# Attention kernel: P by V in blocks of four key tiles instead of two, V made over six steps, and a new order of the first-pass scores

## What is computed

```python
xn = layernorm(x)                                   # (16, 56, 128)
q, k, v = xn @ qw.T + qb, ctx @ kw.T + kb, ctx @ vw.T + vb
scores = einsum('bhqd,bhkd->bhqk', q * 8 ** -0.5, k)
scores = where(mask == 0, -1e9, scores)
out = einsum('bhqk,bhkd->bhqd', softmax(scores), v)
x = x + tanh(g_xattn) * (out @ ow.T + ob)
x = x + tanh(g_ffn) * ffn(layernorm(x))             # 8 experts, top 2, and a shared one
```

## Time and profile before

| | |
|---|---|
| median of 3 runs | 525.68 us (525.66 to 526.95) |
| the profiled execution | 525.51 us, its span 523.7 us |
| PE busy | 473.9 us, 90% of the span |
| PEld busy | 351.7 us, 67% |
| DVE busy | 399.2 us, 76% |
| ACT busy | 329.6 us, 63% |
| POOL busy | 160.5 us, 31% |

### The profile page before, as it was taken

How to read it: one execution, slowest core, us unless ns; L and a number is a source line. 1 busy time by engine, 2 the same in 40 slices (tenths; PEclk the granted TensorE clock), 3 DMA queues, 4 the chain that set the end, 5 groups by cost and what they waited for, 6 DMA issues and landing times.

```text
span 523.7 us, 15766 instructions
## 1 busy us (share of the span) xinstructions
PE 473.9 (90%) x6779; PEld 351.7 (67%) x6779; DVE 399.2 (76%) x784; ACT 329.6 (63%) x422; POOL 160.5 (31%) x142
## 2 busy tenths in 40 slices
PE   1547699999999999999999999999989989999993
PEld 0214377867778686777768677786868856777772
DVE  7339477877877887787788787778867768888776
ACT  2311366666676666667666666766665788877872
POOL 4034326061532606153351615335194200000000
PEclk9959799999999999999999999999999999999998
DMA  5899986996979688796969869684500300221001
GB/s 165 179 254 195 245 193 134 250 200 165 192 173 202 147 184 177 165 199 169 207 134 197 173 162 197 173 171 105 120 3 2 84 2 25 57 73 51 3 1 35
DMA packets 39805, 72.82 MB, mean 139 GB/s; under 512 B 4638, under 2 KB 26271, under 8 KB 39736
## 3 DMA queue, kind: packets, MB, share of 16 engines
q1 hardware_dynamic: 38456, 70.90, 60.6%
q10 hardware_dynamic: 1280, 0.92, 0.7%
HBM read 24.28 MB, written 0.46 MB: 47 GB/s over the span
## 4 chain that ended last, share of the span: by engine, by line
PE 78%; DVE 7%; DMA 5%; ACT 3%; issue 3%; SPq 1%; POOL 1%; ACTq 0%; DVEq 0%
PE ring L342 16%; PE pv L382 16%; PE st L363 11%; PE ring L324 8%; PE ring L286 7%; PE st L858 7%; PE ring L911 6%; DMA ctxT<-in_ctx 4%; DVE max_part L536 2%; ACT v_ext L469 2%; DMA ident_h<-in_c_ident_h 2%; PE pv L911 2%; SPq L268 1%; PE ring L307 1%; PE ring L350 1%
## 5 line engine op out<-in xcount | busy, mean ns | idle before, releaser
L536 DVE TENSOR_REDUCE max_part<-ring 112x1 f32<-112x512 f32 (+1 forms) x384 | 244.9, 675 | 73.4 <-PE ring L342 73.2
L489 ACT ACTIVATE probs<-st 128x896 f32<-128x896 f32 x192 | 172.5, 916 | 73.5 <-PE st L363 71.4
L342 PE MATMUL ring<-keys,qrs 121*112 121x512 f16 (+1 forms) x384 | 149.7, 391 | 6.8 <-DVE max_part L536 3.3
L363 PEld LDWEIGHTS st<-qrs,keys 121*128 121x128 f16 (+1 forms) x1536 | 97.2, 102 | 29.5 <-issue 8.9
L363 PE MATMUL st<-qrs,keys 121*128 121x112 f16 (+1 forms) x1536 | 106.7, 213 | 1.0 <-ACT qrs L478 1.0
L382 PE MATMUL pv<-probs,v_ext 128*32 128x168 f32 (+3 forms) x3072 | 93.6, 262 | 0.1
L382 PEld LDWEIGHTS pv<-probs,v_ext 128*32 128x32 f32 (+1 forms) x3072 | 73.1, 109 | 21.7 <-issue 11.3
L342 PEld LDWEIGHTS ring<-keys,qrs 121*112 121x112 f16 x384 | 49.9, 130 | 41.7 <-DVE max_part L536 17.7
L614 POOL TENSOR_TENSOR k_hi<-k_raw,zero 128x512 f16<-128x512 f32 (+1 forms) x45 | 45.8, 1018 | 86.7 <-ACT k_raw L457 86.7
L286 PE MATMUL ring<-ctxT,w_qkv 128*128 128x512 f32 (+1 forms) x94 | 53.6, 656 | 13.7 <-DMA ctxT<-in_ctx 13.7
L324 PE MATMUL ring<-w_qkv,ctxT 128*128 128x128 f32 (+1 forms) x384 | 60.0, 278 | 1.7 <-ACT v_ext L469 0.5
(11 more groups left out here) (122 smaller groups left out, 352.0 us busy)
## 6 DMA issues: line engine op xcount, KB each, us to landing
ctxT<-in_ctx SPq DMA_DIRECT2D x16, 750.0 KB, 6.2
keys<-mask_add SPq DMA_DIRECT2D x32, 375.0 KB
keys<-k_hi SPq DMA_DIRECT2D x32, 375.0 KB, 6.3
keys<-k_lo SPq DMA_DIRECT2D x32, 375.0 KB, 7.3
keys<-mask_add SPq DMA_DIRECT2D x32, 281.2 KB
mask_raw<-in_mask SPq DMA_DIRECT2D x15, 375.0 KB, 3.5
up_w<-in_up_w SPq DMA_DIRECT2D x9, 256.0 KB, 2.9
down_w<-in_down_w SPq DMA_DIRECT2D x9, 256.0 KB, 3.2
```

The source lines that it names most:

```text
L342: nc.tensor.matmul(ring[0:QW, m % 2, 0:width(c)], qrs[0:ROWS, w, p, :, :].rearrange("r h q -> r (h q)"), keys[0:ROWS, w, p, chunk(c)], sta ...
L363: mm = nc.tensor.matmul(st[0:m, j % 2, p // 4, QW * (p % 4):QW * (p % 4 + 1)], keys[0:ROWS, u, p, j * P:j * P + m], qrs[0:ROWS, u, p, :, : ...
L489: nc.scalar.activation(probs[0:m, j % 4, :].rearrange("p (h c) -> p h c", h=2), st[0:m, j % 2, :, 0:HQ // 2], ACT.Exp).then_inc(s["exps_do ...
L536: nc.vector.tensor_reduce(max_part[:, p, c:c + 1], ring[0:QW, m % 2, 0:width(c)], AX.X, ALU.max).then_inc(s["max_read"], 1)
```

## The change

- `QUAD = 4`: `pe_pv_quad` issues P by V for four tiles at once, at steps 3, 7 and 11, four tiles behind the scores. Step 3 holds the last four tiles of the batch before, and after unit 15 four tiles are left instead of two. `probs` gets eight buffers for it (`PB`), numbered on through the batches.
- V: in units -1 to 13 the halves stand at steps 4, 5, 6 (two), 9 and 10. In unit 14 they stay at 4, 5 and 6, two at each.
- The third V chunk, which now comes after `pe_attn` in the program, waits until the reciprocal has read `misc`. `pe_attn` waits for two stored V chunks in place of three (three in unit 14), and the first K chunk of a unit waits for the stored V of the unit before.
- `S_ORDER` is a new table, `NORM_STEP` is 3 in place of 1, and places 2 and 3 now stand behind the first and the second V group of any step.

```diff
-        probs = sb("probs", [P, 4, HQ])
+        probs = sb("probs", [P, PB, HQ])
...
-        S_ORDER = ((0, 0), (0, 1), (1, 0), (1, 1), (1, 4), (2, 0), (2, 1), (3, 1), (3, 4), (4, 1), (4, 2), (4, 3),
-                   (5, 2), (5, 3), (5, 4), (6, 1), (6, 2), (6, 3), (7, 4), (8, 1), (8, 3), (9, 1), (9, 4), (10, 1))
+        S_ORDER = ((0, 0), (0, 1), (1, 0), (1, 1), (1, 4), (2, 0), (2, 1), (3, 0), (3, 1), (3, 4), (4, 1), (5, 1), (5, 2),
+                   (6, 1), (6, 2), (6, 3), (7, 1), (7, 4), (8, 1), (8, 3), (9, 1), (9, 2), (10, 1), (10, 2))
...
-        K_STEPS, ANY_STEP, V_STEPS, ATTN_STEP, TURN_STEP = (0, 1, 2), 3, (4, 5, 6), 8, 11
-        NORM_STEP, RECIP_STEP = 1, 8
+        K_STEPS, ANY_STEP, ATTN_STEP, TURN_STEP = (0, 1, 2), 3, 8, 11
+        V_LATE = {4: ((0, 0),), 5: ((0, 1),), 6: ((1, 0), (1, 1)), 9: ((2, 0),), 10: ((2, 1),)}
+        V_LAST = {j + 4: ((j, 0), (j, 1)) for j in range(NCH)}
+        NORM_STEP, RECIP_STEP = 3, 8
...
-                elif not known(k, 0):
+                if not known(k, 0):
                     pe.wait_ge(s["v_stored"], NCH * (k + 1))
...
-                pe.wait_ge(s["v_stored"], NCH * (k + 2))
+                pe.wait_ge(s["v_stored"], NCH * (k + 1) + (2 if has(k, 2) else 3))
...
             elif not half:
                 pe.wait_ge(s["v_stored"], NCH * (k + 1) + c)
+                if c == 2 and has(k, -1) and has(k, 2):
+                    pe.wait_ge(s["recip_done"], k)
...
-        LAG = 2
+        LAG = QUAD
-        def pe_pv_pair(pe, b, j):
+        def pe_pv_quad(pe, b, j):
             k, u, t = b
-            if j % 2 and j > LAG and has(k, 0):
-                for i in (j - LAG - 1, j - LAG):
+            if j % QUAD < QUAD - 1:
+                return
+            if j == QUAD - 1 and has(k, -1):
+                for i in range(KT - QUAD, KT):
+                    pe_pv(pe, (k - 1, buf(b, -1), None), i)
+            if j > QUAD and has(k, 0):
+                for i in range(j - 2 * QUAD + 1, j - QUAD + 1):
                     pe_pv(pe, b, i)
-            if j == LAG - 1 and has(k, -1):
-                for i in range(KT - LAG, KT):
-                    pe_pv(pe, (k - 1, buf(b, -1), None), i)
...
-                if j in K_STEPS:
-                    if has(k, 2):
-                        pe_k(pe, b, K_STEPS.index(j))
-                    pe_slot(pe, b, j, 0)
+                if j in K_STEPS and has(k, 2):
+                    pe_k(pe, b, K_STEPS.index(j))
+                pe_slot(pe, b, j, 0)
...
-            if j >= 4 or not known(k, 1):
-                act.wait_ge(s["pv_done"], KT * k + j - 3)
+            if KT * k + j >= PB:
+                act.wait_ge(s["pv_done"], KT * k + j - PB + 1)
```

More of the change, by code:

```diff
@@ L38 @@
 WIDE = CG * HG
+PB = 8
+QUAD = 4
 VPAD = VW * (H - 1) + CW
@@ L209, in lap, with v_steps, slot @@
             return b[2] + (b[1] + off) // NB
+        def v_steps(k):
+            return V_LATE if has(k, 2) else V_LAST
+        def slot(k, j):
+            return (KT * k + j) % PB
         def known(k, below):
@@ L318, in pe_v @@
                     pe.wait_ge(s["recip_done"], k - 1)
+                    pe.wait_ge(s["v_stored"], NCH * (k + 1))
             elif not half:
                 pe.wait_ge(s["v_stored"], NCH * (k + 1) + c)
+                if c == 2 and has(k, -1) and has(k, 2):
+                    pe.wait_ge(s["recip_done"], k)
             for i in range(2 * half, 2 * half + 2):
@@ L383, in pe_pv @@
                                       v_ext[0:m, u, j, VW * h:VW * h + CW],
-                                      probs[0:m, j % 4, S * h:S * (h + n)],
+                                      probs[0:m, slot(k, j), S * h:S * (h + n)],
                                       start=(j == 0 and not last), stop=(j == KT - 1), skip_group_check=True)
@@ L437, in pe_unit @@
                     pe_attn(pe, b)
[L438 to L445, removed]
+                for i in range(2):
+                    for c, half in v_steps(k).get(j, ())[i:i + 1] if has(k, 1) else ():
+                        pe_v(pe, b, c, half)
+                    pe_slot(pe, b, j, 2 + i)
+                pe_pv_quad(pe, b, j)
                 pe_slot(pe, b, j, 4)
@@ L486, in act_exp @@
             act.wait_ge(s["st_made"], KT * k + j + 1)
-            if j >= 4 or not known(k, 1):
-                act.wait_ge(s["pv_done"], KT * k + j - 3)
-            nc.scalar.activation(probs[0:m, j % 4, :].rearrange("p (h c) -> p h c", h=2),
+            if KT * k + j >= PB:
+                act.wait_ge(s["pv_done"], KT * k + j - PB + 1)
+            nc.scalar.activation(probs[0:m, slot(k, j), :].rearrange("p (h c) -> p h c", h=2),
                                  st[0:m, j % 2, :, 0:HQ // 2], ACT.Exp).then_inc(s["exps_done"], 1)
@@ L498, in act_unit @@
                     act_exp(act, b, j)
-                if j in V_STEPS and has(k, 1):
-                    act_v(act, b, V_STEPS.index(j))
+                for c, half in v_steps(k).get(j, ()):
+                    if half and has(k, 1):
+                        act_v(act, b, c)
                 if j == TURN_STEP and has(k, 1):
```

## The result

The changed kernel takes 538.54 us in the median of four runs (537.75 to 539.44), the kernel before 525.67 us beside it: a ratio of 1.024, 95% interval 1.0216 to 1.0264. It is slower by 2.4%. Its profiled execution took 539.44 us, the longest of the four, with a span of 537.6 us.

What follows compares the result with a forecast made beforehand. PE, busy 90% of the span, was taken to bound the kernel. 525.5 + 10.4 (units 1 to 13) - 0.5 + 0.9 + 2.1 (ends) = 538.4 us profiled, given as 538.5; range 532 to 543, own bounds 534 to 542.

Steps and rivals of the forecast that it cites:

- The price of a block: P by V: a block of four takes 1.82 us; three fewer blocks save 0.75 us a unit.
- third rival: Whole kernel: only the blocks' transitions count and no new waits arise, 515.8 us, by the ends 516 to 518; chance 0.02.
- Fifth piece: Steps 0 and 1: the fifth piece waits for the third piece's maximum, a new stall of 0.33 us, and 0.04 behind it.
- eighth: Steps 2 and 3: pieces 7 and 8 are adjacent, so piece 8 stalls 0.35 us, and 0.04 more.
- behind the norm: Steps 4 to 6: the norm delays piece 11's maximum, so piece 13 comes 0.19 us later, and 0.04 more.
- V behind the copied chunk: Steps 4 to 6: the next V half meets the end of ACT's copy; taken as 0.1 us, bound 0.35.
- V's wait for the reciprocal: Steps 8 and 9: V's third chunk waits 1.08 us for DVE's reciprocal, and V then takes 0.11 longer.
- The unit: Units 1 to 13: 23.8 us each against 23.01, taken as +0.8 a unit, +10.4 in thirteen.
- The terms put at nothing: Eight P buffers, the K chunk's wait for stored V, and later V on SP's queue delaying a context load: no cost.
- The ends: Outside units 1 to 13: unit 0 -0.5 us, unit 14 +0.9, unit 15 and the end +2.1.
- the -0.5: Unit 0: fewer blocks -0.75 us, 8 tiles of P by V instead of 10 -0.8, DVE's spacing gives back about 1.0.
- first rival: Steps 8 and 9: the reciprocal's wait hardly bites, so each unit has -0.4 us and the whole takes 523.0; chance 0.06.

Runs made afterwards that it cites:

- run 6: The kernel before with only blocks of four and the norm at step 3, keeping its old piece order and V at steps 4, 5, 6: 541.76 us, ratio 1.0297.
- run 1: The changed kernel with a second, spare reciprocal of the same size on DVE ahead of the used one: 554.63 us, ratio 1.053.
- run 2: The changed kernel with the reciprocal one place earlier in DVE's list, between the two maxima of step 8: 530.98 us, ratio 1.0074.
- Run 8: The kernel of run 7 with unit 15's P by V in pairs again and its norm at step 1: 520.21 us, ratio 0.9887.
- run 3: The changed kernel with the spread sums at step 7 ahead of the block and the reciprocal between step 7's two maxima: 528.48 us, ratio 1.0032.
- run 4: The changed kernel with V back at steps 4, 5 and 6 in every unit, without its wait for the reciprocal: 546.67 us, ratio 1.0372.
- run 9: The kernel of run 7 with P by V in pairs and the norm at step 1: 522.45 us, ratio 0.9925.
- run 7: The changed kernel with a new piece order, none adjacent, spread sums at step 7 and the reciprocal behind two maxima there: 522.58 us, ratio 0.9925.
- run 5: The changed kernel with P by V in pairs again and the norm at step 1, the rest of the change kept: 542.81 us, ratio 1.0311.
- run 10: The kernel of run 8 with one piece moved from step 4, place 2, to step 1, place 4: 516.86 us, ratio 0.9821.

## Why the prediction was right

The forecast was 538.5 us, slower; measured are 538.54. Point by point:

- **The price of a block.** Forecast 1.82 us for four tiles with entry and exit. Measured 312.79 - 310.57 = 2.22 from the piece ahead to the scores behind, less two pieces of 0.20: 1.82. The 0.75 us a unit are saved. The third rival had this saving and no new wait, 515.8 us; run 6 has the blocks without V's move, and the saving is lost again in waits for maxima. The Trainium skill, page "TensorEngine Tiling (Array Packing)", section "Key Properties", says that changing the tiling mode drains the engine. The trace agrees in so far as each block costs 0.25 us beyond its tiles.
- **The small waits.** Fifth piece 0.34 (0.33), eighth 0.33 (0.35), behind the norm 307.92 - 307.31 - 0.44 = 0.17 (0.19), V behind the copied chunk 0.07 (0.1), as a longer V and not as a wait. The piece behind the block of step 7 stands at 312.54 - 296.45 = 16.09 (16.1).
- **V's wait for the reciprocal.** Forecast 1.08 and 0.11, measured 1.17 and 0.08. V starts 3.20 us behind that piece and not 3.11, 0.14 behind the reciprocal's end where I had 0.05. Runs 1 and 2 show that it is this wait and that it follows DVE's list.
- **The unit.** 23.80 us (forecast 23.8), +10.2 in thirteen (+10.4). The terms put at nothing stayed there: PE's printed waits between 58 and 420 us are for the reciprocal, for maxima, for the copied row of maxima in units 14 and 15, and one for a context transfer at the start of unit 0. None is for a P buffer or for stored V ahead of a K chunk, and none for a later context transfer.
- **The ends.** Unit 14 +0.6 (+0.9). Unit 15 +2.1 (+2.1), from the first scores of unit 15 to the last layer 433.79 - 417.60 = 16.19 us (16.2). Run 8 shows that more than half of it is the four-tile blocks, with scores that wait for an exponential to free one of two `st` buffers, and not the two more tiles.
- **What I didn't have**: the start. In the profiled execution the first K chunk of unit 0 comes at 59.60 us and not at 57.38, behind a context transfer that lands later, and the end of unit 0 lies 1.1 us later, where I had 0.5 earlier. Runs 1 and 2 have the same lists as the change up to there, and their first K chunk comes at 58.44 and 57.69, the end of unit 0 at 81.19 and 80.76. So the lateness varies from execution to execution, and at most a part of it is the change's; what makes the transfer late stays open. Unit 0's own length doesn't test the -0.5 either, as its first microseconds run at the lower of the two clock levels, a different number of them each time (mean granted clock in unit 0: 0.91 before, 0.92 after, 0.89 in run 2).

The mechanism held, so it isn't luck that the kernel is slower by some 13 us. That the median meets the forecast to 0.04 us is luck: the four executions lie 1.7 us apart, and on the profiled one, the longest, the forecast of 538.4 is 1.0 us too low, from -0.2 in the thirteen units, -0.3 in unit 14 and +1.6 at the start. The range was also narrower than its own bounds: added up at their ends, 0.9 to 1.2 and 0.8 to 1.5 us a unit and 1 to 4 at the ends give 531 to 547 and not 534 to 542.

The weaker point was the reading of "without the reciprocal's wait -0.4 a unit", the first rival. Runs 3 and 4 are two ways of taking the wait away by itself, and neither reaches it: 23.06 and 24.36 us a unit, not 22.6. In both, a wait taken out of a list where the next waits stand close behind was worth less than its length.

## What to carry to other kernels

Where an engine that sets the time hands pieces to a second one through two buffers, every long block in its list does two things: it costs, and it gives the second engine time to catch up. Before merging blocks, list for each piece the start of the one two before plus the second engine's time, and place the pieces so that this never binds. A new order of the pieces, with V over six steps and the spread sums and their reciprocal moved to step 7, was worth 4 us here with pairs (run 9). The merged blocks added nothing to it in a middle unit (run 7 against 9), and 0.43 us a unit in the change's order (run 5). The best kernel, 9.5 us under the one before, has that order with one piece moved, merged blocks, and pairs in the last unit (run 10); how much of it the merged blocks are is not shown. When an instruction is moved behind something it must now wait for, look at what stands ahead of that on the other engine's list: one place there was 7.7 us.

## What was not expected of the hardware

A wait of PE of 1.17 us a unit leaves the granted clock at 1.00 through all the middle units. With the reciprocal doubled, PE waited 1.9 us (173.3 to 175.2, printed as 1.72) and in four of thirteen units the clock then stood at 0.50 for a little over three microseconds, at 1.66 us each. The thirteen waits are alike (1.72 us as printed, each), and the slow units are every third, the 4th, 7th, 10th and 13th (ends at 180.89, 256.07, 331.25 and 406.44 us, 75.2 us apart), so the wait's length alone does not decide it. What does, no run here shows.
